# Zeroed score rows written by ScalarE, and row numbers made two tiles ahead of their return

## What is computed

```
x = LN(x + mixer(x));        x = LN(x + ternary_ffn(x))      # block 0
x = LN(x + attention1(x));   x = LN(x + moe_top2(x))         # block 1
x = LN(x + attention2(x));   x = LN(x + channel_mlp(x))     # block 2: Win, 16 relus a channel, Wout
x = LN(x + attention3(x));   x = LN(x + expert_ffn(x))       # block 3

# attention: 16 heads of 8 features, scores = q k^T + bias, softmax, times v, output projection
# expert_ffn: top 2 of 8 experts for each token
xe = xf * gate[:, e:e+1];  g, u = split(xe @ gate_up[e].T);  out += (silu(g) * u) @ down[e].T
```

## Time and profile before

| | |
|---|---|
| median of 3 runs | 1231.08 us (1228.68 to 1233.81) |
| profiled execution, its own time | 1231.71 us |
| its span, first to last instruction | 1230.4 us |
| mean granted clock of PE | 0.898 of full speed |
| busy: PE, DVE, ACT, POOL | 1016.9, 785.5, 627.6, 380.9 us |

### The profile page before, as it was taken

The page is one execution under the profiler, slowest core; times in us unless marked ns, Lnnn a source line. Parts: engine busy times, 40 slices in busy tenths (PEclk is TensorE's granted clock), DMA queues, the critical chain, the costliest instruction groups (busy, mean ns, idle before and its releaser), DMA issues.

```text
span 1230.4 us, 18545 instructions
## 1 busy us (share of the span) xinstructions
PE 1016.9 (83%) x6453; PEld 503.6 (41%) x6453; DVE 785.5 (64%) x1543; ACT 627.6 (51%) x1249; POOL 380.9 (31%) x581
## 2 busy tenths in 40 slices
PE   5699889999757699267999999887999999528981
PEld 2366534444445467132333333673222222415541
DVE  5966787777362000688888882578888884654564
ACT  5664446666513344044777776632777778203330
POOL 7536610000127244510000001330111112376564
PEclk9699889999969799676999999886899999759996
DMA  5910334424311220233333210012433220332232
GB/s 144 169 47 1 104 119 147 138 91 121 101 51 37 57 67 12 76 109 119 108 116 104 69 47 1 1 55 83 129 117 132 75 70 1 103 102 57 53 97 70
DMA packets 94933, 101.47 MB, mean 82 GB/s; under 512 B 13000, under 2 KB 76167, under 8 KB 94759
## 3 DMA queue, kind: packets, MB, share of 16 engines
q1 hardware_dynamic: 82729, 89.28, 24.6%
q0 software_dynamic: 6432, 7.97, 2.2%
q10 hardware_dynamic: 5680, 3.04, 0.9%
HBM read 66.60 MB, written 38.09 MB: 85 GB/s over the span
## 4 chain that ended last, share of the span: by engine, by line
PE 61%; DVE 13%; POOL 9%; issue 7%; ACT 6%; DMA 4%; SPq 0%; POOLq 0%; ACTq 0%; DVEq 0%
PE PS L802 14%; PE PS L818 13%; PE PS L775 9%; PE PS L624 5%; PE PS L629 4%; PE PS L926 3%; DVE negm L1479 3%; PE PS L805 2%; PE PS L920 2%; PE PS L778 2%; POOL rows_y L2121 2%; PE PS L826 2%; DVE X L1334 2%; ACT arena L1227 2%; POOL slots L2107 2%
## 5 line engine op out<-in xcount | busy, mean ns | idle before, releaser
L1479 DVE TENSOR_REDUCE negm<-PS 128x2 f32<-128x1024 f32 (+3 forms) x384 | 404.3, 1089 | 88.2 <-PE PS L775 44.5
L1163 ACT ACTIVATE arena<-PS 128x512 f32<-128x512 f32 (+3 forms) x768 | 362.0, 550 | 172.4 <-PE PS L805 112.6
L802 PE MATMUL PS<-arena 128*128 128x512 bf16 (+3 forms) x768 | 235.4, 363 | 7.0 <-ACT arena L1163 6.4
L818 PE MATMUL PS<-arena,VPAD 128*32 128x512 f32 (+3 forms) x1536 | 185.2, 553 | 0.1
L775 PE MATMUL PS<-arena 32*128 32x512 bf16 (+3 forms) x768 | 143.8, 376 | 22.5 <-DVE negm L1479 20.0
L2137 POOL CAST nmp<-negm 128x16 bf16<-128x16 f32 x48 | 9.2, 192 | 392.3 <-DVE negm L1479 255.6
L775 PEld LDWEIGHTS PS<-arena 32*128 32x128 bf16 x768 | 36.3, 91 | 213.4 <-DVE negm L1479 98.0
L802 PEld LDWEIGHTS PS<-arena 128*128 128x128 bf16 x768 | 69.6, 98 | 120.9 <-issue 49.9
L624 PE MATMUL PS<-arena,W 128*128 128x512 f32 x144 | 86.6, 737 | 8.7 <-ACT arena L1088 6.3
L629 PEld LDWEIGHTS PS<-W,arena 128*128 128x128 f32 x672 | 84.5, 204 | 15.8 <-issue 6.9
L629 PE MATMUL PS<-W,arena 128*128 128x128 f32 x672 | 86.9, 290 | 3.9 <-DVE arena L1423 2.0
(11 more groups left out here) (306 smaller groups left out, 1538.5 us busy)
## 6 DMA issues: line engine op xcount, KB each, us to landing
arena<-score_q SPq DMA_DIRECT2D x48, 288.0 KB
arena<-score_k SPq DMA_DIRECT2D x48, 288.0 KB
arena<-max_parts SPq DMA_DIRECT2D x48, 256.0 KB
max_parts<-arena SPq DMA_DIRECT2D x36, 256.0 KB, 2.9
score_k<-arena SPq DMA_DIRECT2D x36, 128.0 KB
score_q<-arena SPq DMA_DIRECT2D x12, 384.0 KB
arena<-rows_y SPq DMA_DIRECT2D x16, 256.0 KB, 4.2
arena<-slots SPq DMA_DIRECT2D x46, 65.0 KB, 1.9
```

The costliest lines, as they stand in the source:

```text
L802: mm = pe.matmul(PS[:, b, q0:S], OK[s][:, r, kt * P:(kt + 1) * P], OQ[s][:, r, q0:S], start=True, stop=True)
L818: mm = pe.matmul(PS[32 * r:32 * r + 32, 7, q0:S], VP[:, u, kt, r, :], PB[:, kt % 2, r, q0:S], start=(kt == 0), stop=True, skip_group_check ...
L1163: act.activation(PB[:, kt % 2, r, q0:S], PS[:, 4 + use % 3, q0:S], ACT.Exp, scale=slope(u % G, r) if o["slope"] else 1.0).then_inc(exped, 1)
L1479: vec.tensor_reduce(negm[:, u % 2, 2 * rp:2 * rp + 2, qt], PS[:, 2 * (use % 2):2 * (use % 2) + 2, 0:nk], AX.X, ALU.max, negate=True).then_ ...
```

## The change

It has two parts. First, the six fills of the large areas move from POOL to ACT, and are no memset there but a copy of one zero column, read 4096 times, over 128 x 4096 fp32. They stand in ACT's list directly ahead of `p.xT` of chunks 0 and 1 in attentions 1 and 3, and behind `void_weights` in attention 2, both in a row. What they wait for stays as it was, and the zero column is waited for as well. Second, POOL makes the row numbers of tile t + 2 in front of the return of tile t; numbers 0 and 1 are made ahead of the loop.

```diff
+AHEAD3 = 2
-BLANK_SLOTS = (-LEAD, -LEAD + 2)
...
+            def blank_rows(a, c):
+                act.wait_ge(*PO.at(WHOLE, "zeros"))
+                act.wait_ge(*(T.at(c, "t.sum"), V.at(c, "cb.tot"), T.at(c, "ch.out"))[a])
+                act.copy(view(arena, lanes[c].big, [2 * R * S]), zeros[:, 0:1].broadcast_to([P, 2 * R * S])).then_inc(blanked[c], 1)
...
                     elif step == "p.xT":
+                        if c < 2:
+                            blank_rows(0, c)
                         evacuate(c, "p1.tr", L.A, L.xT, "p1.xT")
...
                 void_weights()
+                for c in range(2):
+                    blank_rows(1, c)
...
                     elif step == "p.xT":
+                        if c < 2:
+                            blank_rows(2, c)
                         evacuate(c, "p3.tr", L.A, L.xT, "p3.xT")
...
+            def name_of(t):
+                i = t % NTILE
+                if t >= NTILE:
+                    pool.wait_ge(returned3[i], 16 * (t // NTILE))
+                pool.wait_ge(tile_in[i], 16 * (t // NTILE + 1))
+                pool.tensor_scalar(name3[:, i:i + 1], x3[i][:, D + 1:D + 2], 1.0, float(NOWHERE), ALU.mult, ALU.add).then_inc(named3, 1)
+
             def experts3():
+                for t in range(AHEAD3):
+                    name_of(t)
                 for t in range(ALL3):
                     if PARTS3 == 2 and t in END_TILES:
                         norm(END_TILES[t], "e")
-                    if t >= NTILE:
-                        pool.wait_ge(returned3[i], 16 * (t // NTILE))
-                    pool.wait_ge(tile_in[i], 16 * (t // NTILE + 1))
-                    pool.tensor_scalar(name3[:, i:i + 1], x3[i][:, D + 1:D + 2], 1.0, float(NOWHERE), ALU.mult, ALU.add).then_inc(named3, 1)
+                    if t + AHEAD3 < ALL3:
+                        name_of(t + AHEAD3)
                     pool.wait_ge(named3, t + 1)
                     pool.wait_ge(stored3, t + 1)
                     pool.indirect_dma_start(rows_y, ...).then_inc(returned3[t % NTILE], 16)
...
-                def blank_rows_of(c):
-                    pool.wait_ge(*(T.at(c, "t.sum"), V.at(c, "cb.tot"), T.at(c, "ch.out"))[a])
-                    pool.memset(view(arena, lanes[c].big, [2 * R * S]), 0.0).then_inc(blanked[c], 1)
...
                 def slot(t):
-                    if t in BLANK_SLOTS:
-                        blank_rows_of(BLANK_SLOTS.index(t))
```

More of the change, by code:

```diff
@@ L2108, in scatter3 @@
                                                     lanes[c].rows[:, n, j, :], None, bounds_check=SLOTS3 - 1, oob_is_err=False).then_inc(scattered3[g], 16)
+            def name_of(t):
[4 more added lines that the diff above has]
+                pool.tensor_scalar(name3[:, i:i + 1], x3[i][:, D + 1:D + 2], 1.0, float(NOWHERE), ALU.mult, ALU.add).then_inc(named3, 1)
             def experts3():
+                for t in range(AHEAD3):
+                    name_of(t)
                 for t in range(ALL3):
-                    i = t % NTILE
                     if PARTS3 == 2 and t in END_TILES:
                         norm(END_TILES[t], "e")
-                    if t >= NTILE:
-                        pool.wait_ge(returned3[i], 16 * (t // NTILE))
-                    pool.wait_ge(tile_in[i], 16 * (t // NTILE + 1))
-                    pool.tensor_scalar(name3[:, i:i + 1], x3[i][:, D + 1:D + 2], 1.0, float(NOWHERE), ALU.mult, ALU.add).then_inc(named3, 1)
+                    if t + AHEAD3 < ALL3:
+                        name_of(t + AHEAD3)
                     pool.wait_ge(named3, t + 1)
                     pool.wait_ge(stored3, t + 1)
-                    pool.indirect_dma_start(rows_y, bass.IndirectOffsetOnAxis(ap=name3[:, i:i + 1], axis=0), y3[i], None,
-                                            bounds_check=2 * B * S - 1, oob_is_err=False).then_inc(returned3[i], 16)
+                    pool.indirect_dma_start(rows_y, bass.IndirectOffsetOnAxis(ap=name3[:, t % NTILE:t % NTILE + 1], axis=0), y3[t % NTILE], None,
+                                            bounds_check=2 * B * S - 1, oob_is_err=False).then_inc(returned3[t % NTILE], 16)
                 for c in range((PARTS3 - 1) * 2, B):
```

## The result

The changed kernel takes 1221.86 us, the median of 7 runs (1214.67 to 1224.75), the kernel before 1232.13 beside it (7 runs, 1226.46 to 1233.96): a ratio of 0.9922, 95% interval 0.9904 to 0.9941. Forecast were 1221.6 us. The profiled execution has a span of 1220.5 us, 9.9 less than before. One run of a later kernel, f1, took 1898.56 us and is left out of its ratio.

A forecast was written before the change was run, and what follows sets the result against it. No single bound: PE inside the attentions, other engines in their fronts, POOL's returns at the end of the expert stage. From 1231.71 us, +4.0 - 3.0 - 1.6 - 9.5 gave 1221.6 us, range 1217.5 to 1229.0.

The forecast's parts named there:

- attention 1: Front of attention 1: both copies on ACT delay `p.xT`, and the slip stays; +4.0 us (+2.7 to +5.8).
- attention 2: Front of attention 2: normalisations no longer stretched by a memset, both copies just hidden; -3.0 us (-3.3 to -2.4).
- attention 3: Front of attention 3: first copy hidden, second exposed; `split` 2.2 us earlier, term -1.6 us (-2.2 to -1.0).
- expert stage: Returns of tiles on POOL no longer wait for the number just made; -9.5 us (-10.4 to -5.0).
- Both levels are about as likely: Attention 1: PE's clock behind the new hole, full (+2.7 us) or half (+5.8), so +4.0 was taken.
- a sign that it was wrong there: Front of attention 1: a slip beyond 6 us would show the prediction wrong, the clock then to be looked at.
- The gap of 0.30: Expert stage: idle time ahead of a return, 0.30 us instead of 0.77, making a return cost 1.54 us.
- POOL meets PE at tile 11: Expert stage: POOL's returns, 1.54 us apart, catch up with PE's stores at tile 11, then only follow.
- The lag at the end: End of the expert stage: the last return no longer starts late behind the last store; -4.8 us.
- A: Rival, expert stage: the gap ahead of a return does not shrink and POOL keeps 2.01 us; 1230.6 us, chance 0.12.
- B: Rival: ACT bounds all fronts, attention 1 +5.8, attention 2 -1.5, attention 3 0 us; 1226.5 us, chance 0.10.
- C: Rival, fronts: a copy is dearer than its columns say, 7.3 us giving 1239.9 us; chance 0.04.

The follow-up runs named there:

- f1: The changed kernel itself once more, in a session where every kernel took some 20 us more; ratio 0.9913 to the kernel before.
- e2: Against the kernel before, only the six fills as copies on ACT, each row number right ahead of its own return; 1230.88 us, ratio 1.0009.
- e4: The changed kernel with each row number made one tile ahead of its return, not two; 1221.02 us, ratio 0.9920 to the kernel before.
- f2: The changed kernel with two small POOL instructions more ahead of each return, run again beside the changed kernel; ratio 0.9969 to the kernel before.
- e9: The changed kernel with two small POOL instructions more ahead of each return, in the slow session; ratio 0.9965 to the kernel before.
- e10: The changed kernel with the first copy of attention 2 made twice, in the slow session; 1250.23 us, ratio 0.9987 to the kernel before.
- e1: Against the kernel before, only the row numbers made two tiles ahead, the six fills still memsets on POOL; 1220.62 us, ratio 0.9927.
- e8: The changed kernel with attention 1's fills as memsets on POOL and attention 3's second copy behind `p.k/1`; 1211.48 us, ratio 0.9855 to the kernel before.
- e3: The changed kernel with attention 1's two fills back on POOL as memsets in their old slots; 1215.25 us, ratio 0.9880 to the kernel before.

## Why the prediction was right, and which of its terms were off

The mechanisms were right: returns that no longer wait, normalisations that are no longer stretched, copies that are hidden or exposed where the prediction had them. That the total agrees to 0.3 us, 1221.6 against 1221.86, is luck: it hides terms that were off in both directions, and 4.1 us in the profile that nothing touched.

| term | forecast | changed kernel's profile | the other kernels |
|---|---|---|---|
| attention 1 | +4.0 (+2.7 to +5.8) | +6.6 | e2 +5.5, e4 +6.3, f2 +6.6, e9 +4.1, e10 +3.9, f1 +4.3; with memsets e1 and e8 +0.6, e3 -2.9 |
| attention 2 | -3.0 | -3.2 | -3.3 to -3.4 in e2 to e8; with memsets e1 -0.1 |
| attention 3, to `split` | -2.2 | -3.6 | with memsets e1 -1.1 |
| attention 3, 791 to 1050 | -1.6 | -5.3 | -4.2 to -5.5 in the nine others with both copies; with memsets e1 -4.3 |
| expert stage, 1050 to the end | -9.5 (-10.4 to -5.0) | -12.1 | -9.6 to -12.2, mean of eight -10.5; e2 +1.2 |
| what nothing touches | 0 | +4.1 | |

- **Attention 1.** The mechanism was right, the term too small. "Both levels are about as likely" is the step that failed: behind a hole of 2.5 us the projection `p.qk/0` ran at the lower clock in all eight kernels that have copy 0 ahead of `p.xT/0`, 3.50 to 3.75 us, and took 1.88 in the six that do not. The slip of the seven with both copies is 3.9 to 6.6 us, 5.3 in the mean. It falls into two groups by how long the lower clock lasted: the 32 products behind `p.qk/0` took 3.73 to 3.87 us in e9, e10 and f1, little more than in the kernel before (3.73), and up to 4.85 in the others. The +6.6 is also past the 6 us that the prediction had named as a sign that it was wrong there.
- **Attention 2.** Right, with both copies hidden to some 0.1 us, and e10 shows that a third would not be.
- **Attention 3.** The steps were right: copy 0 hidden, copy 1 exposed. Net of what e1 gains with the old memsets, the term is -1.0 (5.3 - 4.3; the mean of all ten kernels with both copies, 5.0, would make it -0.7), against -1.6; the profile from which it was taken had the lower clock there (0.84 against 0.93). It rests on one profile of e1.
- **Expert stage.** The gap of 0.30 was taken from the nearest row and is 0.17; POOL meets PE at tile 11 all the same, in e1 at tile 9. The lag at the end went by 4.6 of the 4.8 forecast, and of PE's waits for loads the 2.7 forecast. Both waits for the inverse roots went whole, 3.7 where 2.9 was counted, and the 0.9 us that DVE was to want back was not. Of the 12.1 in this execution another 1.0 is the first load behind the scatters, which was 2.87 us on its way before and 1.81 here. A mean of 10.5 stands against 9.5.
- **Sum.** With the terms as the experiments have them, 1231.7 + 5.3 - 3.3 - 1.0 - 10.5 = 1222.2. The three fronts add up to +1.0, and e2, which has only them, measured +1.1 us by its ratio (-1.5 to +3.8).
- **Rivals.** A fell: the gap shrank. B was half right: attention 1 was as B had it, attentions 2 and 3 were not. C fell, at 3.60 us a copy.
- **Open:** what two small POOL instructions cost in the session with the long fills, 1.1 us by the profiles or 2.5 to 11.5 by the runs; why e10 missed its ratio and f1 kept its own; and what made SP's fills take longer there.

## What to carry to other kernels

Make what an instruction needs one instruction earlier than right ahead of it: a distance of one gave as much here as two, 0.6 us at each return as long as POOL was behind, some ten returns at the start and a few behind each inverse root; at the pace of the next bound it is worth nothing more. Where a fill moves to another engine, look for the place behind the last urgent step of its chunk, not ahead of the first: three copies moved that way, or left on POOL, made 7 to 8 us more than the change itself (0.9864 and 0.9855 against 0.9922). And profile an unchanged front twice before a term of a few us is read from it: between e1 and e3 the front of attention 1, the same instructions, moved by 3.5 us with the granted clock.

## What had not been expected of the hardware

- The same instructions behind the same hole of 1.78 us ran at a granted clock of 0.50 in one kernel and 1.00 in another (e1 and e3), which changed a front by 3.5 us.
- A return that waits for the POOL instruction right ahead of it starts 0.77 us after that ends; one that doesn't starts 0.17 after it, less than the 0.30 between two scatters (after, e2, e4).
- Behind a hole of 2.48 us the same projection had the lower clock in all eight kernels, but how long that lasted differed: the 32 products behind it took 3.73 us in e9 and e10 and 4.85 in the changed kernel.
- Two small POOL instructions in a row take 0.34 us together (e9), three 0.51 (the changed kernel), one 0.20: behind each other they cost 0.15 each.
